# A masked softmax-weighted sum over 4096 rows: row groups of 2048, 1536 and 512 rows, or of 2048, 1024, 512 and 512

## The chip, the core and the metric
The kernel runs on one core of a Trainium2 chip. The metric is the device time of one execution in microseconds. Engines are called PE (TensorE, with PEld for its weight loads), DVE (VectorE), ACT (ScalarE), POOL (GpSimd) and SP (SyncE, which issues most DMAs).

## What is computed
x is 4096 x 128, adj 4096 x 4096 of int32. A layer norm and a relu give h; H is h times a 128 x 128 matrix plus a bias; each row of the output is x plus an attention average of H over the columns that adj allows. Because the score is a term of the row plus a term of the column, the softmax needs only weights of the columns.

```python
h = jnp.maximum(_layernorm(x, axis=-1), 0.0)
H = h @ W_fc + b_fc
scores = (H @ w_att[:d])[:, None] + (H @ w_att[d:])[None, :] + b_att
scores = jnp.where(adj > 0, scores, -1e9)
out = x + jax.nn.softmax(scores, axis=1) @ H
```

## The kernel before, in words
The softmax over a row's neighbours is the sum of exp(d_j) h_j over the allowed j, divided by the sum of exp(d_j); the row's own term cancels. So the kernel forms weighted rows once (`high` plus `low`, two parts that together keep full precision), multiplies them with a 0/1 mask of adj, and multiplies the 128 x 512 results with the weights W at the end. adj is read once, 64 MB, in an order that the host has laid out.

**Groups, units, pairs.** The 4096 output rows are 8 blocks of 512 (`BLOCK`). `GROUPS` says how many blocks are summed at a time: group 0 has four blocks, group 1 three, group 2 one. Within a group PE walks over the 32 tiles of 128 columns. A unit is the smallest step: one tile times the group's blocks (for a group of one block four tiles), so 2048, 1536 and 2048 mask columns. There are 32 + 32 + 8 = 72 units; `local` is a unit's number within its group. Two units are a pair and come with one DMA from SP into one of four slots of `ring` (L284); the last pair is cut into a half and four quarters (L288, L291). SP issues a pair when both masks of the pair four before it are made (`slot_free`, L267).

**Masks.** DVE turns a unit's integers into a mask (`mask_unit`, L514). In units that are in `SHARED` (n from 20 on, and from the fifth unit of a group) ACT makes the last block's 512 columns (L456). Six masks are kept; a mask waits until `denominators` has been done for the units that used its place (`fours_done`).

**PE.** `sums(n)` (L844, L850) waits for unit n's mask and adds `high` and `low` products into one PSUM bank for each block, a bank that at a new group's start must have been copied out (`sums_copied`, L842). After every four units `denominators` adds the weights alone (L868). At a group's end ACT copies the banks to `sums_T` (L470) and the denominators to `den_rows` (L448); PE turns the latter (`den_columns`, L882), and `products(g, b)` (L892) multiplies block b with W.

**DVE's share at a group's end.** `inverse_of(g)` (L627 to L631) waits for `den_columns`. `result_of(g, b)` first adds the mean of H to rows with no neighbour (L639), then waits for `products_done` and adds the product times the inverse (L646), four instructions each. These calls stand in DVE's program between the masks, at given values of `local`, as do the bias additions (L722, units 36 to 43), `mean_wide` (L739), `mean_H` (L742) and the `fits` chain (L748 to L757) that decides between this path and a general one. Every engine works strictly in its program's order, so a mask that stands behind a waiting instruction waits too. SP stores a block of the output once all loads are issued and `results_ready` says so (L295).

Of the kernel before, what the change touches and what calls it, by code (L numbers as in the profile page):

```python
# [29 lines left out]
GROUPS = [(0, 4), (4, 3), (7, 1)]  # L30
# [17 lines left out]
def gnn_kernel(nc, x, adj_0, adj_1, adj_2, adj, w_fc, w_fc_t_and_a, b_a_b_att, out):  # L48
# [6 lines left out]
    adj_g = [adj_0, adj_1, adj_2]  # L55
# [14 lines left out]
    SHARED = [n for n, u in enumerate(UNITS) if 20 <= n < LAST and n - FIRST[u[0]] >= 4]  # L70
# [4 lines left out]
    def banks_before(g):  # L75
        return sum(w for _, w in GROUPS[:g])

# [3 lines left out]
    with ExitStack() as ctx:  # L81
# [21 lines left out]
        pick = sb("pick", [P, 4], F32)  # L103
        half_steep = sb("half_steep", [P, 1], F32)
# [34 lines left out]
        is_empty = sb("is_empty", [P, len(GROUPS), 16], F32)  # L139
# [75 lines left out]
        products_done = sem("products_done")  # L215
        results_ready = sem("results_ready")
# [45 lines left out]
        def _(sp):  # L262
# [25 lines left out]
            sp.dma_start(ring[:, LAST_PAIR % RING, 0:4 * BLOCK], adj_g[2][3][:, 0:4 * BLOCK]).then_inc(next_to_last_landed, 16)  # L288
            for i in range(PER):
                cols = slice((PER + i) * BLOCK, (PER + i + 1) * BLOCK)  # L290
                sp.dma_start(ring[:, LAST_PAIR % RING, cols], adj_g[2][3][:, cols]).then_inc(last_landed[i], 16)  # L291
# [27 lines left out]
        @block.gpsimd  # L319
        def _(pool):  # L320
            nc.gpsimd.memset(ones_row[:], 1.0).then_inc(ones_ready, 1)
            nc.gpsimd.memset(half_steep[:], -0.5 * STEEP).then_inc(half_steep_ready, 1)
            nc.gpsimd.memset(ident[:], 0.0).then_inc(cleared, 1)
            nc.gpsimd.memset(pick[:], 0.0).then_inc(cleared, 1)
            nc.gpsimd.memset(ones_col[:], 1.0).then_inc(cleared, 1)
            nc.gpsimd.memset(w_cols[:].rearrange("p t c -> p (t c)").bitcast(F32), 0.0).then_inc(cleared, 1)
            pool.wait_ge(w_T_and_a_landed, 16)
            nc.gpsimd.tensor_copy(a_wide[:], a_cols.unsqueeze(2).to_broadcast([P, 2, P])).then_inc(a_wide_ready, 1)
            pool.wait_ge(a_wide_ready, 1)
            pool.wait_ge(cleared, 4)  # L330
            for q in range(4):
                nc.gpsimd.memset(pick[32 * q:32 * q + 32, q:q + 1], 1.0).then_inc(pick_set, 1)
            pool.wait_ge(pick_set, 4)
            nc.gpsimd.affine_select(out=ident[:], in_=ident[:], compare_op=ALU.not_equal, fill=1.0, base=0,
                                    pattern=[[-1, P]], channel_multiplier=1).then_inc(constants_ready, 1)

            for k, (t0, t1) in enumerate(STAGES):
                tiles = slice(t0, t1)
                pool.wait_ge(w_ready, k + 1)
                nc.gpsimd.tensor_copy(w_cols[:, tiles, 0], w_j[:, tiles]).then_inc(pool_chain, 1)  # L340
                pool.wait_ge(pool_chain, 3 * k + 1)
                nc.gpsimd.tensor_tensor(w_rest[:, tiles], w_j[:, tiles], w_cols[:, tiles, 0], ALU.subtract).then_inc(pool_chain, 1)
                pool.wait_ge(pool_chain, 3 * k + 2)
                nc.gpsimd.tensor_copy(w_cols[:, tiles, 1], w_rest[:, tiles]).then_inc(pool_chain, 1)
                pool.wait_ge(pool_chain, 3 * k + 3)
                nc.gpsimd.tensor_tensor(w_cols[:, tiles, 2], w_rest[:, tiles], w_cols[:, tiles, 1], ALU.subtract).then_inc(w_cols_ready, 1)

            pool.wait_ge(neg_min_ready, 1)
            nc.gpsimd.partition_all_reduce(neg_min_all[:], neg_min[:], P, RMAX).then_inc(neg_min_all_ready, 1)

        @block.scalar
        def _(act):
# [107 lines left out]
            for g, (b0, width) in enumerate(GROUPS):  # L460
# [36 lines left out]
        def _(dve):  # L497
# [124 lines left out]
            def inverse_of(g):  # L622
# [4 lines left out]
                nc.vector.tensor_scalar(is_empty[:, g, 0:count], bank[:, SMALL_BANK, 0:count], 0.0, None,  # L627
# [5 lines left out]
            def result_of(g, b, done):  # L633
                b0, width = GROUPS[g]
                k = b0 + b
                for m in range(PER):
                    row = x_sb[:, k * PER + m, :]
                    at = m * width + b
                    last = nc.vector.scalar_tensor_tensor(out=row, in0=mean_H[:], scalar=is_empty[:, g, at:at + 1], in1=row,  # L639
                                                          op0=ALU.mult, op1=ALU.add)  # L640
# [64 lines left out]
            for n in range(20, LAST):  # L705
# [65 lines left out]
            result_of(1, 2, results_ready)  # L771
# [45 lines left out]
        def _(pe):  # L817
# [9 lines left out]
            def sums(n, tiles=None):  # L827
# [6 lines left out]
                for i in tiles or range(step):  # L834
# [5 lines left out]
                    for b in range(width):  # L840
                        if g > 0 and t == 0:
                            pe.wait_ge(sums_copied, banks_before(g - 1) + b + 1)  # L842
                        cols = slice((i * width + b) * BLOCK, (i * width + b + 1) * BLOCK)
                        nc.tensor.matmul(bank[:, b, :], high[:, t, :], mask[:, n % MASKS, cols],  # L844
# [3 lines left out]
                    for b in range(width):  # L848
                        cols = slice((i * width + b) * BLOCK, (i * width + b + 1) * BLOCK)
                        last = nc.tensor.matmul(bank[:, b, :], low[:, t, :], mask[:, n % MASKS, cols],  # L850
# [23 lines left out]
            def den_columns(g):  # L874
                width = GROUPS[g][1]
                rows = 32 * width if width > 1 else P
                of = pick[0:rows, 0:width] if width > 1 else ones_col[:]
# [3 lines left out]
                for m in range(PER):  # L881
                    last = nc.tensor.matmul(bank[:, SMALL_BANK, m * width:(m + 1) * width],  # L882
                                            den_rows[0:rows, m * P:(m + 1) * P], of, start=True, stop=True)
# [12 lines left out]
            for n in range(0, LAST, 2):  # L896
# [10 lines left out]
                if g == 1:  # L907
# [4 lines left out]
                    if local == 2:  # L912
                        pe.wait_ge(row_sum_ready, 1)
                        nc.tensor.matmul(ps_mean, row_sum[:, 0, :], ones_over_n, start=True, stop=True).then_inc(mean_in_psum, 1)
                    if local == 6:
                        pe.wait_ge(mean_wide_ready, 1)
                        nc.tensor.matmul(ps_mean_H, mean_wide[:], w_sb[:], start=True, stop=True).then_inc(mean_H_in_psum, 1)
                    if local in (10, 12, 16, 18):
                        products(0, {10: 0, 12: 1, 16: 2, 18: 3}[local])
                if g == 2:  # L920
                    if local == 0:
                        den_columns(1)
                        products(1, 0)
                        products(1, 1)
                    if local == 4:
                        products(1, 2)
# [60 lines left out]
```

## Time and profile before
| | us |
|---|---|
| three runs: median (lowest to highest) | 186.21 (185.15 to 186.57) |
| the profiled execution, whole | 186.24 |
| its span in the trace | 184.3 |
| busy: PE, DVE, ACT, POOL | 160.3, 124.9, 79.6, 10.7 |
| mean rate of the DMAs | 389 GB/s |

The span runs from the first to the last recorded instruction; the whole time has 1.9 us more around it. PE's busy time is 87% of the span, but a matmul's end is modelled and matmuls overlap, so what a step on PE costs is read from the start of one instruction to the start of the next, or from the chain of waits, which does that. The chain of work that ended last is 59% DMA, 23% PE and 10% DVE. In the timeline a row is a run of like instructions with its start and its length from the first start to the last end; in square brackets stands the idle time before it and what ended that.

### The profile page before, as it was taken

Reading aid. Unit: us, or ns where it says so; the run is one execution under the profiler, and the core shown is the slowest. Engines: PE = TensorE matmul, PEld = TensorE weight load, DVE = VectorE, ACT = ScalarE, POOL = GpSimd, SP = SyncE. Lnnn points to the kernel's source line nnn. Section 1 sums busy time; section 2 is a strip of 40 time slices with the busy share of each in tenths; the row PEclk is TensorE's granted clock in tenths of the full one; section 3 lists DMA queues with packets and bytes.
Section 4 is the critical chain, followed back from the end, with each engine's and each line's share of the span. In section 5 each row is a group of like instructions: output and inputs, shape, how many; then the busy total and the mean of one; then the engine's idle time right before and its main releaser. Section 6 shows DMA issues by size and latency. Waiting matters only on the chain.

```text
span 184.3 us, 2691 instructions
## 1 busy us (share of the span) xinstructions
PE 160.3 (87%) x866; PEld 115.3 (63%) x866; DVE 124.9 (68%) x360; ACT 79.6 (43%) x232; POOL 10.7 (6%) x33
## 2 busy tenths in 40 slices
PE   0639859989499999989899999999999998999970
PEld 0326638666386867656668667686786775887750
DVE  0995696947999556788865569496594624459931
ACT  2567894999395052222251422442224424021020
POOL 2103601000130020000000000000000000000000
PEclk9999987999969999999999999999999999999995
DMA  5999999999999999999999999999999999998212
GB/s 144 410 439 432 412 443 420 434 420 430 427 430 432 412 441 411 441 420 428 420 422 424 427 427 424 422 427 423 425 424 427 437 431 427 411 398 329 76 60 59
DMA packets 8369, 71.63 MB, mean 389 GB/s; under 512 B 929, under 2 KB 1698, under 8 KB 3490
## 3 DMA queue, kind: packets, MB, share of 16 engines
q1 hardware_dynamic: 7776, 71.18, 92.3%
q10 hardware_dynamic: 578, 0.26, 0.5%
q8 instruction: 8, 0.13, 0.3%
q14 instruction: 7, 0.06, 0.1%
HBM read 69.34 MB, written 2.10 MB: 388 GB/s over the span
## 4 chain that ended last, share of the span: by engine, by line
DMA 59%; PE 23%; DVE 10%; issue 2%; ACT 2%; SPq 1%; DVEq 0%
DMA ring<-adj 59%; PE bank L844 9%; PE bank L850 8%; DVE mask L514 5%; PE bank L868 3%; PE bank L892 2%; PE bank L882 1%; DVE low L537 1%; ACT mask L456 1%; DVE mask L523 1%; ACT weighted L363 1%; SPq L271 1%; DVE x_sb L639 1%; DVE x_sb L646 1%; SPq L277 0%
## 5 line engine op out<-in xcount | busy, mean ns | idle before, releaser
L514 DVE TENSOR_SCALAR mask<-ring 128x1024 fp32r<-128x1024 int32 (+2 forms) x69 | 63.1, 934 | 41.6 <-DMA ring<-adj 37.1
L844 PE MATMUL bank<-mask,high 128*128 128x512 f32 x256 | 80.7, 418 | 11.0 <-DVE mask L514 6.3
L850 PE MATMUL bank<-mask,low 128*128 128x512 f32 x256 | 76.3, 401 | 0.0
L844 PEld LDWEIGHTS bank<-mask,high 128*128 128x128 f32 x256 | 47.8, 196 | 31.1 <-DVE mask L514 12.9
L850 PEld LDWEIGHTS bank<-mask,low 128*128 128x128 f32 x256 | 49.8, 194 | 11.1
L456 ACT ACTIVATE mask<-ring,half_steep 128x512 fp32r<-128x512 int32 x43 | 28.9, 718 | 62.1 <-DMA ring<-adj 60.6
L868 PE MATMUL bank<-mask,w_cols 128*32 128x512 bf16 x256 | 19.7, 392 | 2.3 <-ACT lines L422 2.3
L868 PEld LDWEIGHTS bank<-mask,w_cols 128*32 128x32 bf16 x256 | 5.9, 94 | 13.1 <-issue 8.7
L363 ACT ACTIVATE weighted<-relu,w_over_std 128x128 f32<-128x128 f32 x32 | 10.1, 391 | 4.7 <-DVE w_over_std L608 4.5
L374 ACT ACTIVATE relu<-x_sb,neg_mean 128x128 f32<-128x128 f32 x32 | 9.8, 388 | 3.2 <-DVE neg_mean L546 3.2
L389 ACT ACTIVATE high<-x_sb,neg_mean 128x128 fp32r<-128x128 f32 x24 | 9.3, 387 | 0.0
L646 DVE SCALAR_TENSOR_TENSOR x_sb<-bank,inv_den,x_sb 128x128 f32<-128x128 f32 x32 | 9.0, 345 | 0.3
L639 DVE SCALAR_TENSOR_TENSOR x_sb<-mean_H,is_empty,x_sb 128x128 f32<-128x128 f32 x32 | 9.1, 346 | 0.0
L892 PE MATMUL bank<-w_sb,sums_T 128*128 128x128 f32 x64 | 8.6, 280 | 0.0
L892 PEld LDWEIGHTS bank<-w_sb,sums_T 128*128 128x128 f32 x64 | 7.9, 191 | 1.1 <-issue 0.9
L537 DVE SCALAR_TENSOR_TENSOR low<-relu,v_rows 128x128 fp32r<-128x128 f32 x32 | 8.3, 284 | 0.1
L729 DVE SCALAR_TENSOR_TENSOR weighted<-relu,rstd,weighted 128x128 f32<-128x128 f32 x28 | 7.9, 346 | 0.0
L383 ACT ACTIVATE low<-x_sb 128x128 fp32r<-128x128 f32 x24 | 7.1, 296 | 0.0
L470 ACT COPY sums_T<-bank 128x512 f32<-128x512 f32 x8 | 4.2, 597 | 5.9 <-PE bank L850 5.8
L619 DVE TENSOR_TENSOR low<-weighted,high_bits 128x512 fp32r<-128x512 f32 (+2 forms) x10 | 5.9, 586 | 0.3
L369 ACT CAST high<-high_bits 128x512 fp32r<-128x512 f32 (+2 forms) x10 | 5.2, 525 | 1.9 <-DVE high_bits L616 1.8
L722 DVE TENSOR_TENSOR x_sb<-x_sb,lines 128x512 f32<-128x512 f32 x8 | 5.5, 686 | 0.0
(85 smaller groups left out, 67.7 us busy)
## 6 DMA issues: line engine op xcount, KB each, us to landing
ring<-adj SPq DMA_DIRECT2D x18, 2048.0 KB, 17.1
ring<-adj SPq DMA_DIRECT2D x16, 1536.0 KB, 12.9
ring<-adj SPq DMA_DIRECT2D x3, 1024.0 KB, 9.3
out<-x_sb SPq DMA_DIRECT2D x7, 256.0 KB, 13.8
x_sb<-x SPq DMA_DIRECT2D x1, 1024.0 KB, 20.7
ring<-adj SPq DMA_DIRECT2D x4, 256.0 KB, 16.2
x_sb<-x SPq DMA_DIRECT2D x2, 256.0 KB, 3.8
x_sb<-x SPq DMA_DIRECT2D x1, 512.0 KB, 10.1
```

The source lines that it names most:

```text
L363: last = nc.scalar.activation(weighted[:, u % 2, at], relu[:, t, :], ACT.Copy, scale=w_over_std[:, t:t + 1])
L374: nc.scalar.activation(relu[:, t, :], x_sb[:, t, :], ACT.Relu, bias=neg_mean[:, t:t + 1]).then_inc(relu_ready, 1)
L389: nc.scalar.activation(high[:, t, :], x_sb[:, t, :], ACT.Square, bias=neg_mean[:, t:t + 1], accum_out=var[:, t:t + 1]).then_inc(squares_re ...
L456: nc.scalar.activation(mask[:, n % MASKS, cols - BLOCK:cols], ring[:, n // 2 % RING, end - BLOCK:end], ACT.Sigmoid, bias=half_steep[:], sc ...
L514: nc.vector.tensor_scalar(mask[:, n % MASKS, 0:cols], ring[:, n // 2 % RING, begin:begin + cols], 0.0, None, ALU.is_gt).then_inc(masks_rea ...
L537: return nc.vector.scalar_tensor_tensor(out=low[:, t, :], in0=relu[:, t, :], scalar=1.0, in1=v_rows[:, 1, :], op0=ALU.mult, op1=ALU.mult, ...
L639: last = nc.vector.scalar_tensor_tensor(out=row, in0=mean_H[:], scalar=is_empty[:, g, at:at + 1], in1=row, op0=ALU.mult, op1=ALU.add)
L646: last = nc.vector.scalar_tensor_tensor(out=row, in0=bank[:, OUT_BANK + k % 2, m * D:(m + 1) * D], scalar=inv_den[:, col], in1=row, op0=AL ...
L844: nc.tensor.matmul(bank[:, b, :], high[:, t, :], mask[:, n % MASKS, cols], start=(t == 0), stop=False)
L850: last = nc.tensor.matmul(bank[:, b, :], low[:, t, :], mask[:, n % MASKS, cols], start=False, stop=(t == T - 1))
L868: last = nc.tensor.matmul(bank[32 * q:32 * q + 32, DEN_BANK, :], w_cols[:, t, :], mask_16[:, n % MASKS, q * BLOCK:(q + 1) * BLOCK, 1], sta ...
L892: last = nc.tensor.matmul(bank[:, OUT_BANK + k % 2, m * D:(m + 1) * D], sums_T[:, b, m * P:(m + 1) * P], w_sb[:], start=True, stop=True)
```

## The change
Group 1 has two blocks in place of three, and there is a fourth group: blocks 0 to 3, 4 and 5, 6, 7. A unit of group 1 is now two tiles of two blocks, so every unit has 2048 mask columns, every pair 2048 KB, and there are 32 + 16 + 8 + 8 = 64 units. `SUM_BANKS` gives the last two groups PSUM banks 2 and 3, and `bank_free` waits only for the copy that used the bank last. ACT makes the last block's mask from the third unit on in the last two groups. The work between the units is put at other places: the bias additions at units 32 to 35, 45 and 49; mean and mean_H 2 and 4 units after group 1's start in place of 4 and 8; the products of group 0 on PE at local 4, 6, 8, 10 (10, 12, 16, 18 before) and their results on DVE at local 6, 8, 10, 12 (14, 17, 20, 23 before). Products and results of blocks 4 and 5 fall into group 2; in the last group only those of block 6 are left, besides block 7 at the very end.

```diff
-GROUPS = [(0, 4), (4, 3), (7, 1)]
+GROUPS = [(0, 4), (4, 2), (6, 1), (7, 1)]
+
+SUM_BANKS = [[0, 1, 2, 3], [0, 1], [2], [3]]
...
-        step = 4 if width == 1 else 1
+        step = 4 // width
...
-    SHARED = [n for n, u in enumerate(UNITS) if 20 <= n < LAST and n - FIRST[u[0]] >= 4]
+    SHARED = [n for n, u in enumerate(UNITS) if 20 <= n < LAST and n - FIRST[u[0]] >= (4 if u[0] < 2 else 2)]
...
+    def bank_free(g, b):
+
+        for before in range(g - 1, -1, -1):
+            if SUM_BANKS[g][b] in SUM_BANKS[before]:
+                return banks_before(before) + SUM_BANKS[before].index(SUM_BANKS[g][b]) + 1
+        return 0
...
+            nc.gpsimd.memset(pick_two[:], 0.0).then_inc(cleared, 1)
...
+                nc.gpsimd.memset(pick_two[rows, q % 2:q % 2 + 1], 1.0).then_inc(pick_set, 1)
...
-                    nc.scalar.copy(sums_T[:, b, :], bank[:, b, :]).then_inc(sums_copied, 1)
+                    nc.scalar.copy(sums_T[:, b, :], bank[:, SUM_BANKS[g][b], :]).then_inc(sums_copied, 1)
...
+                dve.wait_ge(bias_added, k + 1 if k < PER else 5 if k < 6 else 6)
...
-                if n in range(36, 36 + CHUNKS):
-                    rows = x_sb[:, (n - 36) * PER:(n - 35) * PER, :]
-                    nc.vector.tensor_tensor(rows, rows, b_row.unsqueeze(1).to_broadcast([P, PER, D]), ALU.add)
+                chunks = {32: [0], 33: [1], 34: [2], 35: [3], 45: [4, 5], 49: [6, 7]}.get(n, [])
+                for c in chunks:
+                    rows = x_sb[:, c * PER:(c + 1) * PER, :]
+                    last = nc.vector.tensor_tensor(rows, rows, b_row.unsqueeze(1).to_broadcast([P, PER, D]), ALU.add)
+                if chunks:
+                    last.then_inc(bias_added, 1)
...
-                    if local == 4:
+                    if local == 2:
                         dve.wait_ge(mean_in_psum, 1)
...
-                    if local == 8:
+                    if local == 4:
                         dve.wait_ge(mean_H_in_psum, 1)
                         link(nc.vector.tensor_copy(mean_H[:], ps_mean_H))
                         inverse_of(0)
-                    if local in (14, 17, 20, 23):
-                        result_of(0, (local - 14) // 3, results_ready)
-                    if local == 26:
+                    if local in (6, 8, 10, 12):
+                        result_of(0, (local - 6) // 2, results_ready)
+                    if local == 14:
...
                 if g == 2:
+                    if local == 2:
+                        inverse_of(1)
+                    if local in (3, 5):
+                        result_of(1, (local - 3) // 2, results_ready)
+                if g == 3:
+                    if local == 2:
+                        inverse_of(2)
                     if local == 3:
-                        inverse_of(1)
-                    if local in (4, 5):
-                        result_of(1, local - 4, results_ready)
+                        result_of(2, 0, results_ready)
...
-            result_of(1, 2, results_ready)
...
-                        if g > 0 and t == 0:
-                            pe.wait_ge(sums_copied, banks_before(g - 1) + b + 1)
+                        if t == 0 and bank_free(g, b) > 0:
+                            pe.wait_ge(sums_copied, bank_free(g, b))
...
-                    if local in (10, 12, 16, 18):
-                        products(0, {10: 0, 12: 1, 16: 2, 18: 3}[local])
+                    if local in (4, 6, 8, 10):
+                        products(0, (local - 4) // 2)
                 if g == 2:
                     if local == 0:
                         den_columns(1)
                         products(1, 0)
+                    if local == 2:
                         products(1, 1)
-                    if local == 4:
-                        products(1, 2)
+                if g == 3:
+                    if local == 0:
+                        den_columns(2)
+                        products(2, 0)
```

DVE's program around the results of blocks 0 and 1, in the kernel before (L514 makes a mask, L639 and L646 are the two halves of `result_of`; block 0 is done at local 14, ahead of it are the masks of local 12, 13 and 14):

```order
L514 TENSOR_SCALAR mask<-ring 128x1024 [waits fours_done,pair_landed2] x2
L514 TENSOR_SCALAR mask<-ring 128x1024 [waits fours_done,pair_landed3]
L639 SCALAR_TENSOR_TENSOR x_sb<-mean_H,is_empty,x_sb 128x128 x4
L646 SCALAR_TENSOR_TENSOR x_sb<-bank,inv_den,x_sb 128x128 [waits products_done,vector_chain]
L646 SCALAR_TENSOR_TENSOR x_sb<-bank,inv_den,x_sb 128x128 x3
L514 TENSOR_SCALAR mask<-ring 128x1024 [waits fours_done,pair_landed3]
```

The same engine and place in the changed kernel (L528 makes a mask, L654 and L661 are the two halves; the first mask is unit 38, the second unit 39, the third unit 40):

```order
L528 TENSOR_SCALAR mask<-ring 128x1536 [waits fours_done,pair_landed3]
L654 SCALAR_TENSOR_TENSOR x_sb<-mean_H,is_empty,x_sb 128x128 [waits bias_added]
L654 SCALAR_TENSOR_TENSOR x_sb<-mean_H,is_empty,x_sb 128x128 x3
L661 SCALAR_TENSOR_TENSOR x_sb<-bank,inv_den,x_sb 128x128 [waits products_done,vector_chain]
L661 SCALAR_TENSOR_TENSOR x_sb<-bank,inv_den,x_sb 128x128 x3
L528 TENSOR_SCALAR mask<-ring 128x1536 [waits fours_done,pair_landed3]
L528 TENSOR_SCALAR mask<-ring 128x1536 [waits fours_done,pair_landed0]
```

The result of a block still stands between two masks, but in every pair in place of every third unit. What is new besides is how near its product is on PE. Before, `products(0, 0)` stood behind the unit of local 11, and its result behind the mask of local 14, three units on; for block 1 it is four units (13 and 17). Now `products(0, 0)` stands behind the unit of local 5 and its result behind the mask of local 6, the very next one, and likewise for blocks 1 to 3. In group 1 a call of `products` at an even `local` comes after both units of the pair and after `denominators` where that is due.

PE in the last group, behind its first two units, in the kernel before (L882 is `den_columns`):

```order
L850 MATMUL bank<-mask,low 128x512
L882 MATMUL bank<-pick,den_rows 128x3 x4
L892 MATMUL bank<-w_sb,sums_T 128x128 x8
L844 MATMUL bank<-mask,high 128x512
L850 MATMUL bank<-mask,low 128x512
```

And in the changed kernel:

```order
L872 MATMUL bank<-mask,low 128x512
L903 MATMUL bank<-ones_col,den_rows 128x1 x4
L913 MATMUL bank<-w_sb,sums_T 128x128 x4
L866 MATMUL bank<-mask,high 128x512
L872 MATMUL bank<-mask,low 128x512
```

Eight product matmuls have become four here, and the four of `products(1, 2)`, two pairs further on, are gone from the last group.

## Rows read from the trace of the kernel before

**Rows 1.** Stretches: busy us of PE, PEld, DVE, ACT, POOL; clock, DMA share, GB/s
```profile
120.00:140.00 20.00, 20.00 (x115) 15.39 (x114) 15.59 (x43) 7.16 (x11) 0.00 (x0) 1.00 1.00 423
155.78:176.70 20.92, 20.92 (x128) 16.01 (x128) 14.39 (x37) 2.66 (x4) 0.00 (x0) 1.00 0.75 299
176.70:184.30 7.60, 2.05 (x16) 1.86 (x16) 2.68 (x11) 0.59 (x1) 0.00 (x0) 0.73 0.14 38
```

**Rows 2.** Timeline, masks of pair 15 and of the last group's second pair
```profile
89.60 1.34 ACT L456 ACTIVATE mask<-ring,half_steep 128x512 fp32r<-128x512 int32 x2 [3.56 <-DMA ring<-adj]
89.66 0.96 DVE L514 TENSOR_SCALAR mask<-ring 128x1536 fp32r<-128x1536 int32 x1 [0.84 <-DVE weighted L729]
...
119.11 0.69 DVE L514 TENSOR_SCALAR mask<-ring 128x1024 fp32r<-128x1024 int32 x1 [2.40 <-DMA ring<-adj]
...
159.39 2.36 DVE L514 TENSOR_SCALAR mask<-ring 128x2048 fp32r<-128x2048 int32 x2 [2.53 <-DMA ring<-adj]
```

**Rows 3.** Chain of waits: start us, us, what; from the last group's start
```profile
154.50 1.24 DVE mask L514
...
155.78 0.50 PE bank L844
...
159.72 0.79 PE bank L882 x8
...
166.06 1.02 PE bank L868 x15
167.08 0.43 PE bank L844
...
170.93 0.89 PE bank L892 x8
```

**Rows 4.** Timeline, PE at the start of group 1
```profile
95.79 0.98 PE L844 MATMUL bank<-mask,high 128*128 128x512 f32 x3
```

**Rows 5.** Timeline, mean_H and the inverse between masks 40 and 41
```profile
109.35 1.08 PE L868 MATMUL bank<-mask,w_cols 128*32 128x512 bf16 x12
110.36 0.49 PE L917 MATMUL bank<-w_sb,mean_wide 128*128 128x128 f32 x2
110.60 0.94 PE L844 MATMUL bank<-mask,high 128*128 128x512 f32 x3
110.88 0.29 DVE L742 COPY mean_H<-bank 128x128 f32<-128x128 f32 x1 [1.54 <-PE bank L917]
...
111.79 0.69 DVE L514 TENSOR_SCALAR mask<-ring 128x1024 fp32r<-128x1024 int32 x1
...
112.53 0.96 PE L844 MATMUL bank<-mask,high 128*128 128x512 f32 x3 [0.29 <-DVE mask L514]
```

**Rows 6.** Timeline, DVE at the result of block 0 and the next landings
```profile
119.72 1.14 DVE L639 SCALAR_TENSOR_TENSOR x_sb<-mean_H,is_empty,x_sb 128x128 f32<-128x128 f32 x4
120.90 1.13 DVE L646 SCALAR_TENSOR_TENSOR x_sb<-bank,inv_den,x_sb 128x128 f32<-128x128 f32 x4
121.94 0.69 DVE L514 TENSOR_SCALAR mask<-ring 128x1024 fp32r<-128x1024 int32 x1
...
122.80 1.30 DVE L514 TENSOR_SCALAR mask<-ring 128x1024 fp32r<-128x1024 int32 x2 [0.18 <-DMA ring<-adj]
...
127.46 0.70 DVE L514 TENSOR_SCALAR mask<-ring 128x1024 fp32r<-128x1024 int32 x1 [1.15 <-DMA ring<-adj]
```

**Rows 7.** Costliest groups of the page: busy us, mean ns, idle before and releaser
```profile
L844 PE MATMUL bank<-mask,high 128*128 128x512 f32 x256 | 80.7, 418 | 11.0 <-DVE mask L514 6.3
...
L722 DVE TENSOR_TENSOR x_sb<-x_sb,lines 128x512 f32<-128x512 f32 x8 | 5.5, 686 | 0.0
```

**Rows 8.** Timeline, the fits chain on DVE and the mask behind it
```profile
142.82 0.21 DVE L748 TENSOR_SCALAR fits<-neg_min_all,minus_bound 128x1 f32<-128x1 f32 x1
...
144.23 0.70 DVE L514 TENSOR_SCALAR mask<-ring 128x1024 fp32r<-128x1024 int32 x1
```

**Rows 9.** Timeline, ACT's copies of group 1's banks
```profile
153.55 1.56 ACT L470 COPY sums_T<-bank 128x512 f32<-128x512 f32 x3 [2.61 <-PE bank L850]
```

More of the change, by code:

```diff
@@ L42, in units_of, with gnn_kernel @@
     for g, (_, width) in enumerate(GROUPS):
-        step = 4 if width == 1 else 1
+        step = 4 // width
         out += [(g, t, step) for t in range(0, tiles, step)]
     return out
-def gnn_kernel(nc, x, adj_0, adj_1, adj_2, adj, w_fc, w_fc_t_and_a, b_a_b_att, out):
+def gnn_kernel(nc, x, adj_0, adj_1, adj_2, adj_3, adj, w_fc, w_fc_t_and_a, b_a_b_att, out):
     N, D = x.shape
@@ L626, in inverse_of @@
                     dve.wait_ge(results_ready, GROUPS[g][0])
-                nc.vector.tensor_scalar(is_empty[:, g, 0:count], bank[:, SMALL_BANK, 0:count], 0.0, None,
+                nc.vector.tensor_scalar(is_empty[:, GROUPS[g][0] * PER:GROUPS[g][0] * PER + count], bank[:, SMALL_BANK, 0:count], 0.0, None,
                                         ALU.is_equal)
@@ L635, in result_of @@
                 k = b0 + b
+                dve.wait_ge(bias_added, k + 1 if k < PER else 5 if k < 6 else 6)
                 for m in range(PER):
                     row = x_sb[:, k * PER + m, :]
-                    at = m * width + b
-                    last = nc.vector.scalar_tensor_tensor(out=row, in0=mean_H[:], scalar=is_empty[:, g, at:at + 1], in1=row,
+                    at = b0 * PER + m * width + b
+                    last = nc.vector.scalar_tensor_tensor(out=row, in0=mean_H[:], scalar=is_empty[:, at:at + 1], in1=row,
                                                           op0=ALU.mult, op1=ALU.add)
@@ L840, in sums @@
                     for b in range(width):
-                        if g > 0 and t == 0:
-                            pe.wait_ge(sums_copied, banks_before(g - 1) + b + 1)
+                        if t == 0 and bank_free(g, b) > 0:
+                            pe.wait_ge(sums_copied, bank_free(g, b))
                         cols = slice((i * width + b) * BLOCK, (i * width + b + 1) * BLOCK)
-                        nc.tensor.matmul(bank[:, b, :], high[:, t, :], mask[:, n % MASKS, cols],
+                        nc.tensor.matmul(bank[:, SUM_BANKS[g][b], :], high[:, t, :], mask[:, n % MASKS, cols],
                                          start=(t == 0), stop=False)
@@ L849, in sums @@
                         cols = slice((i * width + b) * BLOCK, (i * width + b + 1) * BLOCK)
-                        last = nc.tensor.matmul(bank[:, b, :], low[:, t, :], mask[:, n % MASKS, cols],
+                        last = nc.tensor.matmul(bank[:, SUM_BANKS[g][b], :], low[:, t, :], mask[:, n % MASKS, cols],
                                                 start=False, stop=(t == T - 1))
@@ L875, in den_columns @@
                 width = GROUPS[g][1]
-                rows = 32 * width if width > 1 else P
-                of = pick[0:rows, 0:width] if width > 1 else ones_col[:]
+                of = {4: pick, 2: pick_two, 1: ones_col}[width][:]
                 pe.wait_ge(den_rows_ready, g + 1)
@@ L882, in den_columns @@
                     last = nc.tensor.matmul(bank[:, SMALL_BANK, m * width:(m + 1) * width],
-                                            den_rows[0:rows, m * P:(m + 1) * P], of, start=True, stop=True)
+                                            den_rows[:, m * P:(m + 1) * P], of, start=True, stop=True)
                 last.then_inc(den_in_psum, 1)
@@ L923, in _ @@
                         products(1, 0)
+                    if local == 2:
                         products(1, 1)
-                    if local == 4:
-                        products(1, 2)
+                if g == 3:
+                    if local == 0:
+                        den_columns(2)
+                        products(2, 0)
             sums(LAST, (PER - 1,))
@@ L972 @@
     for g, (b0, width) in enumerate(GROUPS):
-        step = 4 if width == 1 else 1
-        step *= 2
+        step = 2 * (4 // width)
         part = adj_t[:, :, b0 * BLOCK:(b0 + width) * BLOCK].reshape(tiles // step, step, P, width * BLOCK)
```

19 lines of the change are left out of this document (10 added, 9 removed).

## The prediction
> **What bounds the kernel now.** I read the table of stretches first [rows 1]. From 120 to 140 us the DMA engines are full, at 423 GB/s, and TensorE (PE) is busy too; from 155.78 to 176.70 the DMAs fall to 299 GB/s, and PE is busy for all of the 20.92 us; the last 7.6 us have little of either. The granted TensorE clock is 1.00, the 2.4 GHz level, wherever PE works steadily. So the stream of the adjacency bounds the kernel first, and PE at the end.
>
> The timeline gives the pace of the stream, since a unit's mask starts when its pair lands: pairs of 1536 KB are 3.69 us apart (119.11, 122.80, [rows 2]), pairs of 2048 KB 4.89 (154.50, 159.39, [rows 2, 3]); with pair 15 (mask block at 89.60, [rows 2]) I count 4.91, which is 3.69 x 4/3.
>
> The hand-over is in the chain of waits [rows 3]: at 154.50 VectorE (DVE) makes the first mask of the last group in 1.24, and PE starts at 155.78, after 0.79 of idle time. From there to 176.70 the chain names only PE. Behind it are the last `den_columns`, DVE's last rows and the store; the change touches none of these.
>
> How PE stood before that decides the matter. It started group 1 at 95.79 [rows 4] and is busy for all of 120 to 140 [rows 1]. It has next to no reserve: a microsecond of waiting put into group 1 arrives at 155.78, less the 0.79.
>
> **Prices on PE.** Between the end of the first matmul, 156.28, and 159.72 lie 15 matmuls [rows 3]: 0.229 each, a unit of eight 1.83, one of six 1.37. `denominators` costs 1.02 with 16 matmuls [rows 3] and 1.01 with 12 (109.35 to 110.36, [rows 5]), and the first matmul behind it 0.43 where 0.23 is usual: 1.22 in all, whatever the width. `den_columns` costs 0.79, one `products` 0.89 [rows 3]. A mean matmul costs 0.43 with the slower first one behind it (0.24 from 110.36 to 110.60, [rows 5]).
>
> **The change, part by part.**
> 1. *Last group.* It is the same 8 units in both kernels with the same bytes ahead of it, so its first mask starts at 154.50 again. On PE `products` of three blocks go (3 x 0.89), that of one comes, `den_columns` stays: -1.78. DVE has `inverse_of(2)` and `result_of(2,0)` between masks 58, 59 and 60; by the durations of part 4 mask 60 is ready about 1 us before PE wants it. Zero, and up to 1 if that cover is gone.
> 2. *Start of group 1.* The first pair lands at 89.6 + 4.9 = 94.5; with a mask of 1.24 PE can start at 95.8, as it did. Zero.
> 3. *PE's work from there to the last group.* Now 24 units (44.0), six denominators (7.3), two den_columns (1.6), six products (5.3), the two means (0.9): 59.1. The old list (32 units of six matmuls 44.0, eight denominators 9.8, one den_columns 0.8, four products 3.6, 0.9) gives 59.1 too; with the 0.3 of idle time ahead of 112.53 [rows 5] that ends at 155.2, and the trace has 154.99 (155.78 less 0.79), so this way of counting is 0.2 long. Less that, the new list without any wait ends at 154.7, 1.1 ahead of 155.8.
> 4. *Waits in between*, the term that decides. Before, a block's product was made 3 or 4 units ahead of its `result_of`. Now `products(0,b)` at local 4, 6, 8, 10 is directly followed on PE by the pair of units in whose middle DVE does that very block, and the odd unit's mask is queued behind it on DVE, as the order rows show; PE waits for that mask. Let S be PE's start of the even unit. A DVE copy that waited for a matmul started 0.28 after PE began the next unit (110.60, 110.88, [rows 5]). Then the four additions take 1.04 to the next start (120.90 to 121.94, [rows 6]), the mask 0.96 for 1536 columns [rows 2], the release 0.04 (155.74 to 155.78): the odd unit can start at S + 2.32. PE is through the even one at S + 1.9. Hold 0.4, and 0.1 for the restart (a first matmul of 0.50 against 0.418, the mean of L844, [rows 3, 7]): 0.5, four times: 2.0.
>  *Unit 37*: mean_H and `inverse_of(0)` hold its mask: 0.28 + 0.91 (110.88 to 111.79) + 0.96 + 0.04 = S + 2.19, so 0.4. The kernel before had this hold, the 0.3 of part 3.
>  *Unit 46*: behind mask 45, done at S + 2.28, come two bias additions (1.37 by [rows 7]) and mask 46 (0.96): S + 4.65 with the release, against S + 2.32 + 1.93 for PE: 0.5 with the restart. *Unit 47*: the `fits` chain of 1.41 (142.82 to 144.23, [rows 8]) and a mask, 2.3 against 1.9: 0.45.
>  *Units 34 and 35* get masks just as they are wanted: 0.1 each for the restart.
>  Together 2.0 + 0.4 + 0.5 + 0.45 + 0.2 = 3.55. PE reaches the last group at 154.7 + 3.5 = 158.2 and not at 155.8: +2.4. Bounds: below, nothing is held, and the stream rules (+0). Above, DVE's first four additions, 1.17 (119.72 to 120.90, [rows 6]), are not done when the product is. They start at the landing + 0.96; with PE no later than that, up to 0.9 more is lost once, after which PE is late enough: +3.3. I take +2.4, each step of it being a row of the same operation.
> 5. *Banks of their own.* The wait for `sums_copied` at the last group's start goes. The copies began at 153.55 [rows 9], 2.2 before PE started. Zero.
> 6. *Stream.* 12 x 4.91 = 58.9 for 16 x 3.69 = 59.0: zero. By 153 us six output blocks are ready and go out behind the last load, where four were; 512 KB more at 423 GB/s are at most 1.2 us on loads for which PE, by part 4, comes 2.4 later. GpSimd's new memsets stand at the start, ahead of work with microseconds of room. Zero.
>
> On the stream the Trainium skill gives another answer. Its page "DMA: Bandwidth & Descriptors", section "Anatomy of one DMA", fits a transfer to about 2.0 us fixed plus its bytes at 436 GB/s. By that, four transfers fewer could save up to 8 us. The rows disagree: the time per byte is the same at both sizes, so whatever is fixed is hidden behind the transfers in flight. My sum would stay as it is even by the rule, as PE comes last in it; only rival A would gain, by the 1.1 that PE need not wait: 183.4.
>
> **Sum.** +2.4 - 1.8 = +0.6. The profiled execution took 186.24 for a span of 184.3, and the median is 186.21, so the two are one. Forecast 186.8, which is no change: about 1% is what a measurement of this kernel can tell from none.
>
> **Rivals.**
> *A: the holds don't bite.* If the odd masks are there in time, PE starts the last group with the stream and 1.78 is won: 184.5, 1.0% faster. For it: DVE is idle for much of group 1 (15.6 busy of 20, [rows 1]), and a mask is 0.96 of a 4.9 us pair. Against it: the order of product, result and mask leaves no choice, and the wait for mean_H shows such a hold.
> *B: the holds reach the stream.* A late mask frees its ring slot late. From 122.80 to 127.46 a pair took 4.66 in place of 3.69 [rows 6], the second pair issued after the late mask at 111.79. If each of the four results loses 0.97 like this, landings are 3.9 later, the last group's first mask starts at 158.4, PE at 159.7, 1.5 behind 158.2: 188.3, 1.1% slower. It decides from 2.4 us on. Against it: GB/s in that stretch fell only to 423 [rows 1], and three pairs of 4.9 us are in flight behind the late slot.
> *C: saved products and holds cancel*, 186.2; it lies in the forecast's own range.
>
> **How the numbers follow.** Forecast with C 0.78, own range 185.8 to 187.7 (the last group from 157.2 to 159.1). A 0.14; as its time is right at 1%, 0.10 of it counts as faster. B 0.08, 0.07 of it slower. Same: 0.83. The range takes in A and B: 184.2 to 188.3.
>
> **What would show it.** Right: PE's first matmul of the last group at about 158; PE idle ahead of units 39, 41, 43, 45 for 0.3 to 0.5, released by DVE's mask; a DVE wait ahead of each product's additions; 19.1 from the last group's start to the end of its sums where it was 20.9; pairs 4.9 apart. Wrong: PE starts the last group at 155.8 (A), masks wait for pairs that land well after 154.5 (B), or PE waits in units 48 to 55, for which I have no cause.

## The result, and the profile after
The changed kernel takes 187.34 us (median of 10 runs, 186.99 to 187.98) against 186.00 for the kernel before in the same comparison. The ratio is 1.0078, 95% interval 1.0059 to 1.0097: slower by 0.8%, where I had forecast 0.3% and called it no change. The profiled execution took 187.40, with a span of 185.5.

The table of stretches of the changed kernel, in the columns of [rows 1]:

```profile
120.00:140.00 20.00, 19.21 (x109) 13.36 (x110) 16.03 (x36) 5.34 (x10) 0.00 (x0) 1.00 1.01 426
140.00:155.00 15.00, 15.00 (x90) 12.03 (x89) 10.50 (x26) 3.39 (x6) 0.00 (x0) 1.00 1.01 427
158.51:177.60 19.09, 19.09 (x116) 14.22 (x112) 8.54 (x20) 4.47 (x7) 0.00 (x0) 1.00 0.65 258
177.60:185.50 7.90, 2.05 (x17) 1.86 (x16) 2.68 (x11) 0.58 (x1) 0.00 (x0) 0.69 0.14 37
```

The last group's sums take 19.09 where they took 20.92 [rows 1]. PE, busy for all of 120 to 140 before, has gaps there now, while the DMAs are as full as ever. So the change gave the last group less to do and put waits into group 1. The last group starts at 158.51 and not at 155.78 [rows 3]: +2.73. With -1.83 in the group and +0.3 behind its sums that is the 1.2 between the two profiled executions. (0.18 of the 2.73 is already there when group 1 starts, of which more below.)

The waits in the timeline of PE, ahead of units 39, 41, 43, 45 and 47 (in the bracket the idle time and what ended it):

```profile
113.45 0.73 PE L866 MATMUL bank<-mask,high 128*128 128x512 f32 x2 [0.34 <-DVE mask L528]
...
119.83 0.72 PE L866 MATMUL bank<-mask,high 128*128 128x512 f32 x2 [0.32 <-DVE mask L528]
...
124.99 0.73 PE L866 MATMUL bank<-mask,high 128*128 128x512 f32 x2 [0.30 <-DVE mask L528]
...
131.35 0.73 PE L866 MATMUL bank<-mask,high 128*128 128x512 f32 x2 [0.33 <-DVE mask L528]
...
135.70 0.50 PE L866 MATMUL bank<-mask,high 128*128 128x512 f32 x1 [0.16 <-DVE mask L528]
```

The bracket understates each wait by 0.16, since a matmul is recorded with some 0.39 while the next could start 0.23 after it. The whole of one hold, block 1 between masks 40 and 41, on both engines:

```profile
116.52 1.16 PE L913 MATMUL bank<-w_sb,sums_T 128*128 128x128 f32 x8
117.43 0.71 PE L866 MATMUL bank<-mask,high 128*128 128x512 f32 x2
117.78 1.12 DVE L661 SCALAR_TENSOR_TENSOR x_sb<-bank,inv_den,x_sb 128x128 f32<-128x128 f32 x4 [1.54 <-PE bank L913]
118.83 1.82 DVE L528 TENSOR_SCALAR mask<-ring 128x1536 fp32r<-128x1536 int32 x2
...
119.83 0.72 PE L866 MATMUL bank<-mask,high 128*128 128x512 f32 x2 [0.32 <-DVE mask L528]
```

Unit 40 starts on PE at S = 117.43. DVE has stood still for 1.54, waiting for the product just made, and starts at S + 0.35. The mask of unit 41 begins at S + 1.40, and unit 41 at S + 2.40, where PE could have started it at S + 1.93. The hold is 0.47; I had S + 2.32 and 0.4.

The first of the four holds looks different. Unit 38 starts on PE at S = 111.03, and DVE goes through block 0 without a gap:

```profile
110.23 1.14 DVE L654 SCALAR_TENSOR_TENSOR x_sb<-mean_H,is_empty,x_sb 128x128 f32<-128x128 f32 x4
...
111.40 0.87 DVE L661 SCALAR_TENSOR_TENSOR x_sb<-bank,inv_den,x_sb 128x128 f32<-128x128 f32 x3
```

The additions of the mean end at 111.37 and those of the product start at 111.40 (the view ends at 112, so it shows three of them). That is S + 0.37, as behind the waits, but here DVE's own work since the pair landed at 109.35 lasts just as long. Ahead of unit 39 the trace can't tell the wait for the product from the load of DVE.

### The profile page after: what moved, and what is told of

Read it like the earlier page. It is cut to its first block, busy times and chain, and to the rows that moved or that the text cites. A ratio compares the mean times of both kernels' runs of the same rounds, so it can differ in the third digit from the quotient of the medians.

```text
span 185.5 us, 2673 instructions
## 1 busy us (share of the span) xinstructions
PE 158.3 (85%) x874; PEld 113.0 (61%) x874; DVE 126.1 (68%) x355; ACT 74.8 (40%) x225; POOL 10.8 (6%) x38
## 4 chain that ended last, share of the span: by engine, by line
DMA 47%; PE 29%; DVE 17%; issue 3%; SPq 1%; ACT 1%; DVEq 0%
DMA ring<-adj 47%; PE bank L866 11%; PE bank L872 10%; DVE mask L528 7%; PE bank L890 4%; PE bank L913 3%; DVE x_sb L661 3%; PE bank L903 1%; DVE low L551 1%; DVE x_sb L654 1%; DVE weighted L747 1%; DVE mask L537 1%; ACT weighted L377 1%; SPq L282 1%; DVE x_sb L738 1%
## 5 line engine op out<-in xcount | busy, mean ns | idle before, releaser
L866 PE MATMUL bank<-mask,high 128*128 128x512 f32 x256 | 85.1, 414 | 14.1 <-DVE mask L528 9.2
L528 DVE TENSOR_SCALAR mask<-ring 128x1536 fp32r<-128x1536 int32 (+1 forms) x61 | 64.2, 1069 | 26.8 <-DMA ring<-adj 21.9
L872 PE MATMUL bank<-mask,low 128*128 128x512 f32 x256 | 80.2, 395 | 0.0
L866 PEld LDWEIGHTS bank<-mask,high 128*128 128x128 f32 x256 | 46.4, 192 | 36.2 <-DVE mask L528 19.5
L872 PEld LDWEIGHTS bank<-mask,low 128*128 128x128 f32 x256 | 48.6, 190 | 10.6
L470 ACT ACTIVATE mask<-ring,half_steep 128x512 fp32r<-128x512 int32 x35 | 23.5, 717 | 56.7 <-DMA ring<-adj 48.8
L890 PE MATMUL bank<-mask,w_cols 128*32 128x512 bf16 x256 | 17.6, 392 | 2.3 <-ACT lines L436 2.3
L661 DVE SCALAR_TENSOR_TENSOR x_sb<-bank,inv_den,x_sb 128x128 f32<-128x128 f32 x32 | 9.0, 344 | 5.7 <-PE bank L913 5.6
L890 PEld LDWEIGHTS bank<-mask,w_cols 128*32 128x32 bf16 x256 | 5.4, 94 | 11.9 <-issue 8.0
L641 DVE TENSOR_SCALAR is_empty<-bank 128x4 f32<-128x4 f32 (+2 forms) x4 | 0.7, 166 | 14.4 <-PE bank L903 14.4
L654 DVE SCALAR_TENSOR_TENSOR x_sb<-mean_H,is_empty,x_sb 128x128 f32<-128x128 f32 x32 | 9.1, 346 | 0.0
```

Of the source, the lines that this page charges most:

```text
L470: nc.scalar.activation(mask[:, n % MASKS, cols - BLOCK:cols], ring[:, n // 2 % RING, end - BLOCK:end], ACT.Sigmoid, bias=half_steep[:], sc ...
L528: nc.vector.tensor_scalar(mask[:, n % MASKS, 0:cols], ring[:, n // 2 % RING, begin:begin + cols], 0.0, None, ALU.is_gt).then_inc(masks_rea ...
L661: last = nc.vector.scalar_tensor_tensor(out=row, in0=bank[:, OUT_BANK + k % 2, m * D:(m + 1) * D], scalar=inv_den[:, col], in1=row, op0=AL ...
L866: nc.tensor.matmul(bank[:, SUM_BANKS[g][b], :], high[:, t, :], mask[:, n % MASKS, cols], start=(t == 0), stop=False)
L872: last = nc.tensor.matmul(bank[:, SUM_BANKS[g][b], :], low[:, t, :], mask[:, n % MASKS, cols], start=False, stop=(t == T - 1))
L890: last = nc.tensor.matmul(bank[32 * q:32 * q + 32, DEN_BANK, :], w_cols[:, t, :], mask_16[:, n % MASKS, q * BLOCK:(q + 1) * BLOCK, 1], sta ...
```

## The experiments
Two numbers of each run are compared. One is the start of PE's first matmul in the last group, "the start". The other is the time from there to the start of the last matmul of the sums, "the stretch". Before they are 155.78 and 20.52, in the changed kernel 158.51 and 18.70. Each start is that of one profiled execution, and executions differ already where the programs are the same: group 1 started between 95.61 and 96.28 in the eight kernels with the new groups, and at 95.79 and 95.86 in the two with the old ones. Times are medians, each ratio is against the kernel before on the same chip. In the experiments that derive from the changed kernel the lines of DVE's results and masks keep its numbers or are a few off.

**Results behind the odd mask.** All that changes is where DVE does the results of blocks 0 to 3:

```diff
-                    if local in (6, 8, 10, 12):
-                        result_of(0, (local - 6) // 2, results_ready)
+                    if local in (7, 9, 11, 13):
+                        result_of(0, (local - 7) // 2, results_ready)
```

> The changed kernel with the results of blocks 0 to 3 one unit later (local 7, 9, 11, 13), so behind the odd mask. Theory (holds): PE no longer waits 0.46 to 0.50 ahead of units 39, 41, 43, 45 plus 0.1 for each restart, 2.4 in all, and mask 46 and 47 get ahead too: the last group's first matmul at 155.3 to 155.8 (was 158.5), time 184.3 (185.0 at most). Rival (larger units and earlier bookkeeping cost it anyhow): the first matmul stays at 158 or later, time 187.3. Rival (stream): the same, since pairs land as before.

185.29 us, ratio 0.9971 (0.9953 to 0.9989). Start 156.01, stretch 18.69. One unit's move of four calls took back 2.5 of the 2.73; counted from the start of group 1, which came at 95.73 here and at 95.97 in the changed kernel, it is 2.26 of 2.55. The waits at 39, 41, 43 and 45 are gone; DVE makes both masks of a pair and then the result, which has its product by then:

```profile
109.10 1.83 DVE L528 TENSOR_SCALAR mask<-ring 128x1536 fp32r<-128x1536 int32 x2 [1.13 <-DMA ring<-adj]
110.85 1.13 DVE L654 SCALAR_TENSOR_TENSOR x_sb<-mean_H,is_empty,x_sb 128x128 f32<-128x128 f32 x4
112.02 1.13 DVE L661 SCALAR_TENSOR_TENSOR x_sb<-bank,inv_den,x_sb 128x128 f32<-128x128 f32 x4
113.99 1.83 DVE L528 TENSOR_SCALAR mask<-ring 128x1536 fp32r<-128x1536 int32 x2 [0.85 <-DMA ring<-adj]
```

Two waits were left, which I had expected to vanish, so that the start came 0.2 to 0.7 later than expected and the time missed the 185.0:

```profile
130.91 0.73 PE L866 MATMUL bank<-mask,high 128*128 128x512 f32 x2 [0.18 <-DVE mask L528]
133.19 0.73 PE L866 MATMUL bank<-mask,high 128*128 128x512 f32 x2 [0.17 <-DVE mask L528]
```

They are units 46 and 47. Behind mask 45 stand the bias additions and now also block 3's result, and behind mask 46 the `fits` chain.

**The other work too.**

```diff
-                chunks = {32: [0], 33: [1], 34: [2], 35: [3], 45: [4, 5], 49: [6, 7]}.get(n, [])
+                chunks = {32: [0], 33: [1], 34: [2], 35: [3], 47: [4, 5], 49: [6, 7]}.get(n, [])
...
-                    if local == 4:
+                    if local == 5:
                         dve.wait_ge(mean_H_in_psum, 1)
...
-                    if local == 14:
+                    if local == 15:
```

with the results as in the run before.

> As the one before, and mean_H with inverse_of(0) at local 5, the bias of blocks 4 and 5 at unit 47 and the fits chain at local 15, each behind an odd mask. Theory: the 0.3 ahead of unit 37 goes too and nothing is left ahead of 46 and 47; the stream then sets the last group's start, 155.2 to 155.5, time 184.2, which is 1.0% under the kernel before. If PE is not held any more and still starts later than 156, something else in group 1 costs time.

184.59 us, ratio 0.9935 (0.9912 to 0.9958): 2.75 under the changed kernel and faster than the kernel before, if by 0.65% and not by 1.0%. Start 155.45, stretch 18.69. PE still waits at 130.58 and 135.73, but DVE's other work had no part in it: both masks had themselves waited for their pair (129.57, 134.45).

```profile
129.57 1.83 DVE L528 TENSOR_SCALAR mask<-ring 128x1536 fp32r<-128x1536 int32 x2 [0.86 <-DMA ring<-adj]
```

```profile
130.58 0.73 PE L866 MATMUL bank<-mask,high 128*128 128x512 f32 x2 [0.33 <-DVE mask L528]
...
135.73 0.50 PE L866 MATMUL bank<-mask,high 128*128 128x512 f32 x1 [0.19 <-DVE mask L528]
```

So the stream is the bound up to unit 48. From 135.73 on PE has only its own list, and it comes to the last group 0.15 behind the stream: the first mask starts at 154.02, which would have let PE start at 155.30, and the denominators ahead of it take their usual 1.02.

```profile
154.02 2.36 DVE L528 TENSOR_SCALAR mask<-ring 128x2048 fp32r<-128x2048 int32 x2 [3.06 <-DMA ring<-adj]
```

```profile
154.43 1.09 PE L890 MATMUL bank<-mask,w_cols 128*32 128x512 bf16 x16
155.45 0.50 PE L866 MATMUL bank<-mask,high 128*128 128x512 f32 x1
```

Stream and PE are even there.

**Results a pair later, still between the masks of a pair.** This separates the wait for the product from the time that DVE is busy.

```diff
-                    if local in (6, 8, 10, 12):
-                        result_of(0, (local - 6) // 2, results_ready)
-                    if local == 14:
+                    if local in (8, 10, 12, 14):
+                        result_of(0, (local - 8) // 2, results_ready)
+                    if local == 15:
```

> The changed kernel with the results of blocks 0 to 3 a pair later (local 8, 10, 12, 14), still between the two masks of a pair, and the fits chain at local 15. The product is then long there, so DVE waits for nothing but is busy for 2.2 between the masks. Theory: a hold needs the late start of the wait; PE is behind by over 2 us, so units 41 to 45 are held 0 to 0.2 each, unit 47 by up to 0.9 (bias, result and mask behind one another); last group at 156 to 157, time 185.0 to 185.9. Rival (the time DVE takes between the masks is what matters, not the wait): holds of 0.5 at 41, 43, 45, 47 as before, time 187.3.

185.87 us, ratio 1.0003 (0.9986 to 1.0019). Start 156.60. From 112 on one recorded wait is left, at unit 47, with about the size expected:

```profile
133.78 0.73 PE L866 MATMUL bank<-mask,high 128*128 128x512 f32 x2 [0.89 <-DVE mask L528]
```

DVE does the same 2.2 us between two masks as in the changed kernel; with the product long there, units 41, 43 and 45 have no recorded wait. For these three it is the wait for a product made a moment ago that holds the mask, and not DVE's load. The load leaves little room, though: mask 43 is ready at 123.20 and PE takes it at 123.23, while masks 41 and 45 are 0.4 and 1.0 early. Unit 39, whose pair has no result in this run, is not tested by it, and the wait left at unit 47 is one of landing and load: the pair landed at 129.68, 0.42 after DVE was through with the bias additions, and mask 46, the result and mask 47 follow without a gap.

**The hold made longer.** Results one unit earlier, ahead of the even mask:

```diff
-                    if local in (6, 8, 10, 12):
-                        result_of(0, (local - 6) // 2, results_ready)
+                    if local in (5, 7, 9, 11):
+                        result_of(0, (local - 5) // 2, results_ready)
```

> The changed kernel with the results of blocks 0 to 3 one unit earlier (local 5, 7, 9, 11), so ahead of the even mask and right behind the product. Theory: PE waits from the end of each product for the rest of the result and one mask, 0.28 + 1.04 + 0.96 + 0.04 = 2.3 and 0.1, four times, where it was 0.6: 7.2 more, last group at 165.7, time 194.5. If the hold is absorbed elsewhere (PE's lag behind the stream), less than half of that, under 191.

197.58 us, ratio 1.0627 (1.0595 to 1.0659). Start 168.69, which is 10.2 later than in the changed kernel (0.3 of it before group 1 starts); I had expected 7.2. The holds have the size expected, 0.16 above the bracket's 2.15 to 2.28:

```profile
113.76 0.73 PE L866 MATMUL bank<-mask,high 128*128 128x512 f32 x2 [2.15 <-DVE mask L528]
...
123.56 0.73 PE L866 MATMUL bank<-mask,high 128*128 128x512 f32 x2 [2.16 <-DVE mask L528]
...
130.66 0.73 PE L866 MATMUL bank<-mask,high 128*128 128x512 f32 x2 [2.28 <-DVE mask L528]
...
140.47 0.73 PE L866 MATMUL bank<-mask,high 128*128 128x512 f32 x2 [2.16 <-DVE mask L528]
```

The other 3.0 are TensorE's clock, in the last column but two:

```profile
110.00:114.00 4.00, 1.85 (x13) 1.53 (x12) 2.28 (x6) 0.99 (x2) 0.00 (x0) 1.00 1.00 426
...
115.20:118.00 2.80, 2.80 (x8) 2.12 (x8) 0.43 (x2) 0.69 (x2) 0.00 (x0) 0.50 1.03 433
...
138.00:142.00 4.00, 1.84 (x10) 1.39 (x10) 3.58 (x8) 0.67 (x2) 0.00 (x0) 1.00 0.05 20
```

Behind the first hold the granted clock fell to 0.50, the 1.2 GHz level, and rows of two matmuls that start 0.46 apart otherwise are 0.86 apart:

```profile
115.36 1.05 PE L872 MATMUL bank<-mask,low 128*128 128x512 f32 x2
116.22 1.05 PE L866 MATMUL bank<-mask,high 128*128 128x512 f32 x2
```

Eight matmuls take 3.3 there (115.36 to 118.67) where 1.83 is usual. It fell again behind the third, and not behind the second and the fourth. In windows of 4 us from 114 to 122 and 130 to 138 the clock was 0.64, 0.93, 0.77 and 0.80, 3.4 us' worth of full speed missing. The last row shows rival B's mechanism: with DVE this late the stream ran dry, 20 GB/s from 138 to 142. In the changed kernel it did not.

**The banks shared again.**

```diff
-SUM_BANKS = [[0, 1, 2, 3], [0, 1], [2], [3]]
+SUM_BANKS = [[0, 1, 2, 3], [0, 1], [0], [0]]
```

> The changed kernel with SUM_BANKS [[0, 1, 2, 3], [0, 1], [0], [0]], so that the last two groups use bank 0 again and PE waits for the copy out of it. My prediction: the copy (0.6) is done under the denominators (1.02), no wait, 187.3, within 0.2 of the changed kernel. Rival (the own banks are what helps): each of the two starts waits for up to two copies, 0.6 to 1.2, of which all arrives at the end: 188 to 189.

187.26 us, ratio 1.0073 (1.0045 to 1.0100), as the changed kernel; start 158.45. The own banks change nothing that can be measured.

**Late products in the kernel before.**

```diff
-                    if local in (10, 12, 16, 18):
-                        products(0, {10: 0, 12: 1, 16: 2, 18: 3}[local])
+                    if local in (12, 14, 18, 20):
+                        products(0, {12: 0, 14: 1, 18: 2, 20: 3}[local])
```

> The kernel before with the products of blocks 0 to 3 at local 12, 14, 18, 20 in place of 10, 12, 16, 18, so that those of blocks 0 and 2 stand directly ahead of the units between whose masks their results are made. Theory (holds against PE's reserve): two holds of 0.28 + 1.04 + 0.69 + 0.04 - 1.47 = 0.58 and 0.1 each, 1.4, less the 0.8 that PE idles ahead of the last group: +0.6, last group at 156.3 and no idle time ahead of it, 186.4 against 185.8. Rival (only the group's split matters): 185.8.

186.45 us against 185.85, ratio 1.0036 (1.0018 to 1.0055). Start 156.62, stretch 20.51. The two holds are there:

```profile
123.73 0.96 PE L844 MATMUL bank<-mask,high 128*128 128x512 f32 x3 [0.51 <-DVE mask L514]
...
136.99 0.96 PE L844 MATMUL bank<-mask,high 128*128 128x512 f32 x3 [0.49 <-DVE mask L514]
```

and the idle time ahead of the last group, 0.79 in [rows 3]'s kernel, is gone. With the old groups, the nearness of product and result alone costs 0.6, and the reserve takes up the rest of the 1.5.

**What the work taken from the last group is worth.** In the kernel with everything behind odd masks I put one product and its result back.

```diff
                         products(1, 0)
-                    if local == 2:
-                        products(1, 1)
                 if g == 3:
                     if local == 0:
+                        products(1, 1)
+                    if local == 2:
                         den_columns(2)
                         products(2, 0)
```

with DVE's `result_of(1, 1)` at local 1 of the last group, `inverse_of(2)` at 4 and `result_of(2, 0)` at 5.

> The kernel with everything behind the odd masks (184.6), but products(1,1) and its result back in the last group, and den_columns(2), products(2,0) and their inverse and result a pair later. This undoes half of what the change takes from the last group. Theory: that group takes 0.89 longer, 19.9 to 20.0, and starts at most 0.3 earlier, at the stream's 155.2: +0.6 to +0.9, 185.2 to 185.5. If PE's work in the last group is not what sets the end, 184.6 again.

189.47 us, ratio 1.0173 (1.0121 to 1.0225): start 155.28, stretch 23.89. This is a miss of my making. At local 1 the result stands ahead of mask 58 and directly behind its product, which is the hold of the changed kernel again, 2.15 of recorded idle time. The clock is down behind it here too (0.84, 0.73 and then 1.00):

```profile
160.00:164.00 4.00, 1.85 (x6) 1.41 (x6) 3.08 (x7) 2.52 (x5) 0.00 (x0) 0.84 0.97 400
164.00:168.00 4.00, 4.00 (x20) 2.83 (x23) 0.74 (x1) 1.12 (x2) 0.00 (x0) 0.73 1.05 398
168.00:172.00 4.00, 4.00 (x38) 3.21 (x31) 2.09 (x8) 0.72 (x1) 0.00 (x0) 1.00 0.57 220
```

Without that fault:

```diff
-                        act.wait_ge(products_done, b0)
+                        act.wait_ge(products_done, 5 if g == 2 else b0)
...
                 if g == 3:
-                    if local == 1:
+                    if local == 3:
                         result_of(1, 1, results_ready)
```

> The run before had a hold of its own that I had overlooked: result_of(1,1) stood ahead of mask 58 and right behind its product. Here it stands behind mask 59 (local 3), and ACT's copy of block 6 waits only for products(1,0), the last reader of its buffer, so that ACT's part of mask 58 isn't late either. Theory: no wait of PE ahead of units 58 and 59 and no fall of the clock; the last group takes 0.89 longer than in the kernel with everything behind odd masks (19.9 against 19.05) and starts at 155.2 to 155.5: 185.2 to 185.5 against 184.6. Rival (work put back in the last group is hidden): 184.6.

185.60 us, ratio 0.9985 (0.9969 to 1.0001). Start 155.52, stretch 19.95, which is 1.26 longer than 18.69; the time is 1.0 longer (0.9 by the two ratios). I had 0.89. The chain of waits has 0.89 for the first product and 1.00 for the other, 0.98 for `den_columns` behind `denominators`:

```profile
159.45 0.89 PE bank L915 x8
164.08 1.02 PE bank L892 x15
165.10 0.98 PE bank L905 x8
166.09 1.00 PE bank L915 x8
```

Each step between unlike matmuls costs some 0.1, which my price for a product leaves out. That the work put back is hidden, at 184.6, is excluded: product work in the last group does arrive at the end in full.

## Why the prediction was right, and where it was off
- *Last group, -1.78*: measured 19.09 against 20.92, -1.83. The cover of part 1 held: PE waited for no mask there.
- *Start of group 1, zero*: PE started it at 95.97 and not at 95.79 [rows 4], +0.18. Kernels with the very same program up to there started it anywhere from 95.61 to 96.28, so this is the spread of single executions and not the change.
- *PE's own work, equal to the old list's within the method's 0.2*: consistent with the kernel that moved everything. PE is on the stream there up to 135.73, so the 154.7 that I gave for a list without any wait wasn't tested as a whole. The part from unit 48 on was: by my prices (eight units, two denominators, one `den_columns`, two products) it takes 19.65, and it took 19.72, with one restart in it.
- *Waits, +3.55*: from starts of units in the changed kernel, the four results hold 0.46 to 0.49 each, and the first matmul behind a wait is 0.1 late. Unit 37 (108.28 for 108.01) had 0.27, unit 46 0.14 and unit 47 0.35, all before the restarts. Unit 46 was over-priced at 0.4, the others within 0.1. The mechanism is shown by three runs for units 41, 43 and 45: one unit's move took back all four holds, a product made early enough took these three away with DVE just as busy, and a longer hold had its computed length. For unit 39 it is in part argued. One sign failed there, a DVE wait ahead of each product's additions: block 0 had none, since DVE's additions of the mean ended (111.37) just as the product was ready. That is also the edge of my upper bound, in which they end later still and up to 0.9 more is lost; nothing of it was.
- *Start of the last group, 158.2*: measured 158.51. The 0.3 missing is the later start of group 1 (0.18) and 0.1 that I can't place.
- *The sum* came out low, +0.6 for +1.34 between medians (+1.16 between profiled executions; the one before, 186.24, lies 0.24 above its median). Beside the 0.3 just named, "the change touches none of these" failed by 0.3: from the end of the sums to the end of the span it is 7.90 in the changed kernel and 7.6 before, though DVE's last row ends 3.9 behind the sums in both. The difference lies in the last stores. It was 7.7 to 8.1 in all runs that derive from the changed kernel and 7.1 in the one that derives from the kernel before. The two with the old groups are thus 0.5 apart themselves, and how much of the 0.3 belongs to the change stays open, as does its cause. Both errors of 0.3 went the same way, and the stated range was wide enough for them.
- *Banks, zero*: right, by the run that shares them.
- *Stream, zero*: pairs land 4.9 apart (99.56, 104.46, 109.35, 114.23), and the last group's first mask starts at 153.86, 0.6 earlier than the 154.50 before. Little of that is the change: in the six other kernels with the new groups whose stream never ran dry the mask starts at 154.00 to 154.31, and in the other one with the old groups at 154.21. In the changed kernel the gain meets a PE that starts 3.4 us later than this mask would let it. The saving of up to 8 us that I had worked out in the prediction, as an estimate from the Trainium skill's page "DMA: Bandwidth & Descriptors" (section "Anatomy of one DMA — SWDGE (gpsimd) path"), doesn't show: four transfers fewer, and at most 0.6. The page gives that fit for transfers issued by GpSimd and these are issued by SP, so the runs don't contradict it as it stands there.
- *Rivals*: A's 184.5 is what comes out with everything behind the odd masks (184.59); with the four results alone moved it is 185.29. B's mechanism exists, but needed holds of 2.3 each. The slow pair of [rows 6] on which I based its price is something else: in the kernel with everything behind the odd masks no mask of that stage is late, and still a pair comes 5.86 behind the last (118.81, 124.67) where 4.9 is usual, with the DMAs at 422 GB/s or more all the while. What delays it stays open.

```profile
124.67 1.83 DVE L528 TENSOR_SCALAR mask<-ring 128x1536 fp32r<-128x1536 int32 x2 [1.82 <-DMA ring<-adj]
```

- *Rival C*, the two cancelling, has the wrong size: the measured interval begins at +0.6%.
- *The clock*: "1.00 wherever PE works steadily" holds in both kernels from 56 us to the end of the sums. In group 0 of the kernel before it fell twice, as the last section shows. It changed no term of the sum, since PE waits for masks again at 80.88 and 90.67, before group 1.

## What to carry to other kernels
Moving work off the last stretch pays only if what is moved does not stand between a producer and the next piece that another engine waits for. Where an engine with a strict order does side work, put it behind the last item that others need soon, and put a waiting instruction at least a unit behind what it waits for: here one step of four calls was worth 2.1 us (187.34 against 185.29), more than the 1.8 that the change saves in the last group. An engine that is "busy 87%" with a reserve of 0.8 us is a place where each tenth has to be counted from start to start.

## What the runs showed of the hardware that I had not expected
The clock. In none of the ten traces was a recorded idle time of PE of up to 1.9 us by itself followed by a fall of the granted clock. Those of 2.1 to 2.4 us were followed, or joined in their last tenths, by 3 to 4 us at the 1.2 GHz level in three of the five cases that the experiments made, at a price of about 1.5 us each on top of the wait: 3.0 for two in the run with longer holds, and in the run with the product put back 3.9 (23.89 against 19.95) for one, of which the wait itself is 2.4. Group 0 has such idle times in every kernel too, at about 25 and 51 us and in two kernels at 42. With them it is 13 of 27. (One of 4.3 to 4.7 us at 12 us, when PE has done little yet, is in every trace and was never followed by a fall.) In the kernel before the clock fell behind both of its two, which the stretches show with 0.83 and 0.91:

```profile
20.00:30.00 10.00, 7.67 (x39) 5.41 (x38) 6.72 (x36) 8.59 (x42) 2.10 (x8) 0.83 1.02 433
...
40.00:60.00 20.00, 16.66 (x86) 11.61 (x86) 18.36 (x66) 14.63 (x51) 2.53 (x4) 0.91 1.01 427
```

```profile
25.10 1.08 PE L868 MATMUL bank<-mask,w_cols 128*32 128x512 bf16 x16 [2.33 <-ACT lines L422]
```

In the changed kernel there are three (2.32, 2.44 and 2.12), and it fell behind none. Which of two equal idle times is followed by the drop can't be told from these rows, so a hold of this size is a cost that comes and goes.
